# Cross-attention on one core: GpSimd adds the two weighted V rows of its three groups, VectorE accumulates nine rows per tile instead of twelve

## What is computed

```python
Q, K, V = heads(query, Wq), heads(key, Wk), heads(value, Wv)     # 16 heads of 32
Ks, Vs = ([K], [V])
while Ks[-1].shape[2] > 1:                                       # the tree: 512 + 256 + ... + 1 nodes
    ...
    Ks.append(0.5 * (k2[:, :, :, 0] + k2[:, :, :, 1]))
    Vs.append(v2[:, :, :, 0] + v2[:, :, :, 1])
nk, nv = flatK[:, :, idx_table], flatV[:, :, idx_table]          # 12 nodes per row
self_logits = einsum('bhnd,bhnd->bhn', Q, K) * scale
nbr_logits = einsum('bhld,bhlnd->bhln', Q, nk) * scale
w = softmax(concat([self_logits[..., None], nbr_logits], -1))    # 13 weights per row and head
out = einsum('bhln,bhlnd->bhld', w, concat([V[:, :, :, None, :], nv], 3))
out = out @ Wo.T + bo
```

## Time and profile before

| | |
|---|---|
| median of three runs | 2287.67 us (2282.79 to 2293.26) |
| the profiled execution | 2283.89 us |
| its span in the profile | 2282.0 us |
| busy in the span: TensorE, VectorE, ScalarE, GpSimd | 1983.7, 1854.0, 1057.0, 1126.6 us |
| granted TensorE clock, mean | 0.95 of full speed |
| gathers (line 1690), in all | 384, 371.5 us of GpSimd |
| GpSimd's multiplies of V (line 1718) | 96, 182.6 us |
| VectorE's accumulates (line 1500) | 384, 268.2 us |

### The profile page before, as it was taken

One profiled execution on the slowest core, in us unless ns is written; L12 is line 12 of the kernel. 1 busy time (PEld: TensorE's weight loads), 2 busy tenths in 40 slices (PEclk: granted clock), 3 DMA queues, 4 the chain that ended last, 5 costly groups with the idle time before them and its releaser, 6 DMA issues.

```text
span 2282.0 us, 34451 instructions
## 1 busy us (share of the span) xinstructions
PE 1983.7 (87%) x11744; PEld 1042.1 (46%) x11744; DVE 1854.0 (81%) x2416; ACT 1057.0 (46%) x1854; POOL 1126.6 (49%) x1132
## 2 busy tenths in 40 slices
PE   5599999899999999876259998999999999989997
PEld 2244444344443444322125555555555555555555
DVE  7579888889898898877688888888888888888940
ACT  3255555455555555545114444444444444444443
POOL 3325555445364556363545645555546546456520
PEclk9799999999999999988569999999999999999999
DMA  5334343444444444434856657567567566576520
GB/s 181 115 119 137 121 140 113 153 130 150 138 130 148 129 129 139 128 124 172 273 188 234 220 188 256 194 208 257 181 232 245 198 222 234 194 246 221 198 75 19
DMA packets 188809, 392.51 MB, mean 172 GB/s; under 512 B 20692, under 2 KB 82260, under 8 KB 188632
## 3 DMA queue, kind: packets, MB, share of 16 engines
q1 hardware_dynamic: 133336, 188.91, 25.8%
q0 software_dynamic: 55296, 201.35, 25.4%
HBM read 312.33 MB, written 77.59 MB: 171 GB/s over the span
## 4 chain that ended last, share of the span: by engine, by line
DVE 25%; PE 9%; DMA 6%; POOL 5%; issue 5%; ACT 1%; DVEq 0%; POOLq 0%; ACTq 0%
DVE e_ps L1500 7%; DMA inputs<-kv_flat,idx_rows 6%; DVE swapped L1447 5%; DVE inputs L1496 5%; DVE inputs L1438 4%; POOL inputs L1690 3%; PE aux L899 3%; POOL inputs L1718 2%; PE o_ps L923 2%; PE misc_ps L923 1%; PE e_ps L859 1%; PE rows_ps L859 1%; DVE e_ps L1506 1%; DVE total L1477 1%; DVE swapped L1451 1%
## 5 line engine op out<-in xcount | busy, mean ns | idle before, releaser
L1690 POOL DMA_INDIRECT inputs<-kv_flat,idx_rows x384 | 371.5, 967 | 136.6 <-issue 93.7
L1374 DVE TENSOR_REDUCE neg_max<-rows_ps 128x1 f32<-128x512 f32 x512 | 326.5, 679 | 88.3 <-PE rows_ps L783 82.7
L728 PE MATMUL aux<-inputs 128*128 128x512 f16 x1536 | 356.9, 385 | 32.8 <-POOL inputs L1601 21.8
L899 PE MATMUL aux<-probs,queries 128*128 128x256 f16 x2048 | 356.2, 276 | 0.7 <-issue 0.7
L1500 DVE TENSOR_TENSOR e_ps<-e_ps,inputs 128x512 f32<-128x512 f32 x384 | 268.2, 698 | 42.6 <-POOL inputs L1718 20.9
L1101 ACT ACTIVATE probs<-e_ps 128x1024 f32<-128x1024 f32 x256 | 261.8, 1023 | 76.1 <-PE e_ps L815 75.5
L1718 POOL TENSOR_TENSOR inputs<-inputs,split_up 128x1024 f32<-128x1024 f32 x96 | 182.6, 1915 | 211.5 <-DVE split_up L1484 210.8
L899 PE MATMUL aux<-probs,keys 128*128 128x256 f16 x1024 | 281.8, 275 | 0.0
L728 PEld LDWEIGHTS aux<-inputs 128*128 128x128 f16 x1536 | 150.6, 99 | 218.0 <-POOL inputs L1601 21.8
L1415 DVE TENSOR_TENSOR probs<-probs 128x2048 f32<-128x2048 f32 x96 | 229.2, 2387 | 19.3 <-ACT probs L1101 19.2
L1447 DVE TENSOR_REDUCE swapped<-inputs 128x32 f32<-128x1024 f32 x192 | 229.8, 1211 | 0.0
(11 more groups left out here) (164 smaller groups left out, 3437.0 us busy)
## 6 DMA issues: line engine op xcount, KB each, us to landing
kv_flat<-nodes SPq DMA_DIRECT2D x128, 256.0 KB
nodes<-kv_flat SPq DMA_DIRECT2D x32, 512.0 KB
queries<-qk_dram SPq DMA_DIRECT2D x96, 128.0 KB, 2.7
keys<-qk_dram SPq DMA_DIRECT2D x96, 128.0 KB, 3.0
split_up<-in_pieces SPq DMA_DIRECT2D x40, 256.0 KB
inputs<-in_xT SPq DMA_DIRECT2D x8, 1024.0 KB, 6.3
inputs<-in_ctxT SPq DMA_DIRECT2D x8, 1024.0 KB, 7.5
qk_dram<-high SPq DMA_DIRECT2D x32, 256.0 KB, 2.2
```

Source lines behind the costliest of these rows:

```text
L728: mm = pe.matmul(o[:], w_part[:, w, c, f], x_part[:, which, c, :], start=c + k == 0, stop=c == KC - 1 and k == 2)
L899: mm = pe.matmul(HB[c % 2][:, 0:RW], w[:, k, c * P:(c + 1) * P], x_part[:, k, half * RW:(half + 1) * RW], start=k + i == 0, stop=k == KC - ...
L1374: dve.tensor_reduce(neg_max[:, g % 2, at + i:at + i + 1], rows_ps[:, i, :], AX.X, ALU.max, negate=True).then_inc(max_done, 1)
L1690: pool.indirect_dma_start(nb[:, slot(lt, g), k, :], None, rows, bass.IndirectOffsetOnAxis(idx_rows[:, lt, at:at + 1], 0))\
```

## The change

The groups that GpSimd multiplies (3, 4 and 5) count one row for the accumulation, not two: behind each multiply GpSimd waits for its own result, by a new semaphore `v_mul_part`, and adds the second weighted row to the first. VectorE adds one row per such group. `O_STEPS` falls from 13 to 10, and the gathers and `load_own` wait for the counts that go with it.

```diff
-O_STEPS = 1 + NN
...
+ROWS_OF = tuple(1 if g in POOL_V_GROUPS else GN for g in range(NG))
+O_STEPS = 1 + sum(ROWS_OF)
...
+            v_mul_part = sem("v_mul_part")
...
                     def accumulate(g, k):
-                        dve.wait_ge(o_part, START + n * O_STEPS + 1 + g * GN + k)
+                        dve.wait_ge(o_part, START + n * O_STEPS + 1 + sum(ROWS_OF[:g]) + k)
                         dve.tensor_tensor(ROW[:], ROW[:], nb[:, slot(lt, g), k, D:2 * D], ALU.add).then_inc(o_part, 1)
...
                         accumulate(g, 0)
                         if g + 1 in DVE_V_GROUPS:
                             multiply(g + 1)
-                        accumulate(g, 1)
+                        if g not in POOL_V_GROUPS:
+                            accumulate(g, 1)
...
-                    return b * (TT * O_STEPS) + i // NG * O_STEPS + 1 + GN * (i % NG + 1)
+                    return b * (TT * O_STEPS) + i // NG * O_STEPS + 1 + sum(ROWS_OF[:i % NG + 1])
...
                         w = weights[:, g * GN:(g + 1) * GN, :].unsqueeze(3).to_broadcast([P, GN, H, DH])
-                        pool.tensor_tensor(vv, vv, w, ALU.mult).then_inc(v_mul_pool, 1)
+                        pool.tensor_tensor(vv, vv, w, ALU.mult).then_inc(v_mul_part, 1)
+                        n = (b * TT + lt) * len(POOL_V_GROUPS) + POOL_V_GROUPS.index(g)
+                        pool.wait_ge(v_mul_part, START + n + 1)
+                        rows = nb[:, slot(lt, g), :, D:2 * D]
+                        pool.tensor_tensor(rows[:, 0, :], rows[:, 0, :], rows[:, 1, :], ALU.add).then_inc(v_mul_pool, 1)
```

## The result

| | before | after |
|---|---|---|
| median | 2286.37 us (4 runs, 2282.79 to 2293.26) | 2384.83 us (4 runs, 2378.05 to 2389.69) |
| ratio | | 1.0409, 95% interval 1.0376 to 1.0442 |
| profiled execution, span | 2282.0 us | 2376.2 us |
| first to last start of the weights' line | 1101.7 to 2187.6: 1085.9 us | 1096.6 to 2283.8: 1187.1 us |

The kernel is 4.1% slower. The forecast was 2386 us. The last line of the table is the cross stage alone: 31 periods from the start of the weights of tile 0 to that of tile 31. It is 101.2 us longer, while the spans differ by 94.2: the part ahead of the first tile was 5.1 us shorter in this execution, which the change doesn't touch, and the part behind the last tile about 2 us shorter.

What follows compares the result with a forecast made beforehand. The prediction took GpSimd's late gathers, which VectorE and then TensorE follow, as the bound. 104.4 us for 30 tiles, +4.0 for tile 0, −3.9 and −2.3 gave +102.2 on 2283.9: 2386 us, range 2345 to 2425.

Steps and rivals of the forecast that it cites:

- The loop: Cross stage: GpSimd's group 5 work, its gathers, then VectorE set each tile; 1 us later there lengthens the tile 1 us.
- rows 7's kind: Tiles with the index update, 14 of 30: first gather 0.85 us behind the update's cast, nothing hidden, GpSimd's end 4.05 us later.
- The add: GpSimd, three per tile: 1.27 us each plus 0.08 us wait for its own multiply, together 1.35 us.
- The rival of contended adds: VectorE's work slows GpSimd's adds, each with its wait passing 1.79 us; 2427 us, chance 6%.
- The cover: 16 tiles without index update: 1.07 us of the first two adds hidden behind group 0's sum, GpSimd's end 2.98 us later.
- Nothing for VectorE's saving: VectorE's three saved accumulates, 2.28 us per tile, gain nil in gather-gated tiles; only 3.9 and 2.3 us count elsewhere.
- the waits for gathers stay near 100 us: Expected sign on VectorE: waits for gathered rows about as before; shrinking by more than 20 us would show the forecast wrong.
- The accumulate saved behind P: VectorE's third saved accumulate, after GpSimd's group 5 work: its gain is lost in the wait for the next gather.
- The sum: Whole kernel: 104.4 + 4.0 − 3.9 − 2.3 = +102.2 us on 2283.9, so 2386 us; chance 78%.
- From S to S: S is the end of a tile's weights (line 1484), from which GpSimd starts; the period before was 34.3 us.
- the waits for the query, which gave the 3.9: VectorE's seven waits for TensorE's query, 5.5 us in all, shrink by 0.7 us each where long enough: −3.9 us.
- what follows the last S: Last tile, where nothing is gathered: all three saved accumulates count, −2.3 us.

Runs made afterwards that it cites:

- e2_nine_rows_no_add: The change without GpSimd's adds: VectorE accumulates nine rows and three second rows are left out of the sum; 2282.89 us, ratio 0.9985 to the kernel before.
- e1_twelve_rows: The kernel before plus the three adds on GpSimd, written to an unread place, VectorE still accumulating twelve rows; 2401.43 us, ratio 1.0496 to the kernel before.
- e5_after_index_late: The change with the index update moved from ahead of the first gather to behind the eighth; 2376.13 us, ratio 1.0356 to the kernel before.

## Why the prediction was right

*The loop.* The reading that a tile's length is P + 10.2 + 12 us, P being GpSimd's end on group 5, held in the direction of this change. P moved by 2.98 us in tiles without the index update and by about 4.05 in those with it (16.2 for 12.2 us in the tile of rows 7's kind), and the tiles by 3.3 us on average. Forecast were periods of 37.3 and 38.4 us; measured were 37.3 (the mean of 37.53 and 37.06 for lt 0 and 1) and 38.6 (38.82 and 38.46). The forecast took 34.3 us as the period before for both; it was 34.4 and 34.9, so the tiles grew by 2.9 and 3.8 us, a little less than P.

*The add.* 1.27 us forecast, 1.270 measured, with a spread of 20 ns. The residual add's quiet value was the right one, its mean was not: VectorE's work in the two stages differs, and the multiply of line 1718 told which stage slows GpSimd. The Trainium skill (GPSIMD Engine Reference, "Elementwise — side-by-side cycle accounting") has 4497 ns for an add of 2048 elements, and a quarter of it, 1.12 us, was an estimate; the measurement is 13% above that. The wait for the own result is 0.08 us (1875.85 to 1875.93). The rival of contended adds fell.

*The cover.* The 1.07 us hidden behind group 0's sum in 16 tiles, nothing in 14: both seen in the first gathers, 6.73 and 8.2 us after S for 6.8 and 8.1.

*Nothing for VectorE's saving.* Right in kind (e2_nine_rows_no_add), a little too strict in size: I allowed 6.2 us, e1_twelve_rows gives 10 to 20, the surplus in part at the query.

*What I had wrong beside the sum.* I wrote that the waits for gathers stay near 100 us and that the one for GpSimd reaches 130 or more. They are 117.3 (128.2 with "issue") and 167.6; the second is no contradiction, the first is. The accumulate saved behind P had to show there, 0.7 us in each of 30 tiles, as my own sentence on it said; I didn't carry it over to the list. TensorE's stretch also costs a little more than its share told: its granted clock falls from 0.97 to 0.93 in the stretch, and its busy time for the same work rises from 1983.7 to 2009.7 us, since it now stands idle 4.4 us ahead of line 842 in the tile shown, for 2.7 ahead of line 840 before, and then runs matmuls at 0.63 instead of 0.38 us for about 5 us (to 1895.9), for about 2 before (to 1829.6). That stays off the path here: VectorE waits for the query only 3.0 us in all.

*The sum.* +102.2 forecast, +98.5 between the medians, +101.2 in the stage. From S to S, the tiles 1 to 30 grew by 98.7 us together for 100.5 in the sum (104.4 − 3.9), tile 0 by 2.5 for 4.0 (the waits for the query, which gave the 3.9, fell by 2.5), and what follows the last S shrank by 1.9 for 2.3. So every term has the right sign and about the right size; that the total hit within 2 us of the median, from a base 2.5 us below it, is in part luck.

*What the forecast did not need, and would have got wrong:* the same rule the other way. Issuing the eighth gather earlier by 1.25 or 2 us brought 8 us each time instead of 30 or 36, and about 4 of the 8 come with the late index update. The transfers and the query stood within a microsecond or two of the issue.

## What to carry to other kernels

A share of busy time, 54% for GpSimd here, says nothing on whether work can be moved there: ask what the engine issues behind the place where the work is put, and who waits for it; here each microsecond ahead of the gathers was one in the tile. Test a relief by itself first: a kernel with VectorE's nine accumulates and no adds shows in one run that there is nothing to gain. And with a loop bound by waits, look for what starts it late (here the order of two accumulates, 26 to 28 us, and the order of two projections, 12 us) before moving work between engines; where two or three paths are within a microsecond, delays cost in full and advances only as far as the next path.

## What the runs showed of the hardware

- GpSimd starts a gather 0.14 to 0.18 us behind a compute instruction when the semaphores for it were passed while that instruction ran (0.16 behind a multiply before, 0.15 behind an add after), and 0.84 to 0.85 us behind the index cast, whose own result the gather waits for; so it was ahead of the first gather and, once moved, ahead of the ninth (e5_after_index_late). A short instruction whose result the gather needs therefore costs its own time and some 0.7 us more.
- Gathers of 512 KB issued 1.24 us apart queue: from the start of the eighth to its use it is 6.4 us, 7.8 when GpSimd makes no pause between them, and 4.4 and 5.2 with 256 KB each. The mean busy share of the DMA engines from 10 to 20 us behind S is 0.92, 0.97, 0.65 and 0.79 in the same order. The issue rate of GpSimd alone doesn't tell when rows arrive.
- In the kernel with the shorter gathers and three multiplies ahead, TensorE raised `h_rest` 3.6 to 9.8 us after the recorded end of the matmul of line 906 in 14 of 256 places, and 0.014 us after it in the median. In the kernel before ScalarE waits likewise in 14 places ahead of line 1167, 65.1 us in all, with no releaser named, each time for a semaphore that only TensorE raises, and that rose 2.3 to 2.4 us after the recorded end. A wait without a named releaser can so be one for TensorE. What holds TensorE is left open.
